# Softmax attention: the relative bias reaches the maxima through VectorE, the key tiles take another order, and the relative product is issued behind S^T

## The chip, the cores and the metric

The kernel runs on one core of a Trainium2 chip. The metric is the device time of one execution in microseconds (us). It is one launch of a two-layer network; the change touches only the softmax attention of the second layer.

## What is computed

Each layer adds an attention and a mixture of experts to its input. The attention of the second layer has 2 batches of 16 heads of size 8 over 1024 tokens, with a relative bias that depends on the clipped distance of key and query:

```
q, k, v = x @ Wq.T, x @ Wk.T, x @ Wv.T            # per head, size 8
att_rel_pos = einsum('bhsd,pd->bhsp', q, pos_emb_k)
att_idxs = clip(key - query, -128, 127) % 256
att_pos = att_rel_pos[:, :, query, att_idxs]
att = softmax((q @ k.T + att_pos) / sqrt(8), axis=-1)
y = (att @ v) @ Wproj.T
```

The distance is clipped at 128, so outside a band of three tiles of 128 keys around each tile of 128 queries the bias is one number per query and side. The kernel puts that constant into the product itself (two versions of the keys, `ka` and `kb`, one for either side) and adds the part that varies only inside the band.

## The kernel before

`softmax_attention` walks 256 slots, 16 for each of 16 pairs of heads. Three jobs run in each slot, shifted against each other.

- **R**, the relative product of row `r = n + 26` (`offsets`, L855): 24 rows by 384 columns into `rel_ps`. ScalarE copies it to `rel_sb` (L967). SyncE writes it to memory (L762) and reads it back skewed into `rel_raw` (L775), a ring of 16 rows.
- **S**, the scores of slot `m = n + 14` (`scores`, L873): a tile of 128 queries against half of the keys, two heads of 512 columns, in one of three pairs of PSUM banks (`duo`). VectorE takes the maximum of each head's 512 columns (L1009) into `part`. After 8 slots L1014 joins the two halves to `negmax`, TensorE turns it (L954), VectorE saves it (L1020), and SyncE writes it as a 25th row of `q`.
- **T**, the transposed scores S^T of slot `n` (`turned`, L900): a tile of 128 keys, in the order of `KEYS`, against half of the queries. The 25th row takes the maximum off. `turned_band` (L912) adds the band by transposing pieces of `rel_raw`. ScalarE takes the exponential (L971), and two slots later `values` (L927) multiplies it with v.

S needs the bias before its maximum. Before, `scores_band` (L887) did this on TensorE, ahead of the scores: an identity product of `rel_raw` into the banks of the next slot's S, and the scores were added on top. 10 of 16 slots have such a band, of 1 to 3 tiles for each head; in T 10 of 16 slots have one too, of 2, 4 or 6 transposes.

The banks are handed out in the order S, T, S, T over three pairs. So T of a slot waits until VectorE has reduced S of the slot before, and S waits for the exponential of two slots before (`free_pair`, L840). TensorE's order in a slot is R, S, T, T's bands, S's bands for the next slot, values. R, S and T use 24 or 25 rows of the array, in a quarter of it that depends on the head and on whether the pair is even or odd; for slots 6 to 15 of a pair R lies in the same quarters as T, for 2 to 5 in the same as S. The experts' gate choice (`choose`) is cut into steps that VectorE does in every second slot at the start.

Of the kernel before, what the change touches and what calls it, by code (L numbers as in the profile page):

```python
# [22 lines left out]
P = 128  # L23
# [623 lines left out]
def softmax_attention(nc, d, sb, scr, router):  # L647
# [9 lines left out]
    RING = 16  # L657
    KEYS = ((5, 0, 6, 1, 7, 2, 4, 3), (4, 0, 5, 1, 6, 2, 7, 3))
    with ExitStack() as ctx:
        def tile(name, shape, dt=F32):  # L660
            return ctx.enter_context(nc.sbuf_tensor("a1_" + name, shape, dt))

        def sem(name):
# [7 lines left out]
        rel_raw = tile("rel_raw", [P, RING, 2, BAND])  # L671
        part = tile("part", [P, 2, 2, 2, 4])
        negmax = tile("negmax", [P, 2, 2, 4])
# [12 lines left out]
                                                                sem("zeroed"), sem("ones_ready"))  # L686
        guarded = sem("guarded")
        qk_loaded = [sem(f"qk_loaded{s}") for s in range(4)]
# [36 lines left out]
        def bank_pair(kind, index):  # L725
            return duo[job_of[kind, index] % 3]

        banks = [duo[c // 2][:, c % 2 * CH:(c % 2 + 1) * CH] for c in range(NC)]
# [60 lines left out]
        def _(pool):  # L789
# [4 lines left out]
            pool.memset(f32(kb[:]), 1.0).then_inc(ones_ready, 1)  # L794
            pool.memset(vs[:], 0.0).then_inc(cleared, 1)
            pool.wait_ge(cleared, 2)
            pool.memset(vs[:, :, :, :, HD:2 * HD], 1.0).then_inc(cleared, 1)
# [40 lines left out]
        def _(pe):  # L838
# [18 lines left out]

            def has_band(j, x):
                return max(j - 1, 4 * x) < min(j + 2, 4 * x + 4)

            def scores(m):
                pair, j, x = m // 16, m % 16 // 2, m % 2
                out = bank_pair("s", m)
                edge = min(max(j + 2, 4 * x), 4 * x + 4)
                fresh = not has_band(j, x)
                if fresh:
                    free_pair("s", m)
                for kv, a, b in ((kb, edge, 4 * x + 4), (ka, 4 * x, edge)):
                    if a < b:
                        for hd in range(2):  # L870
                            to = rows(pair, hd, K3)
                            at = hd * CH - 4 * x * P
                            ins = pe.matmul(out[:, at + a * P:at + b * P], qs[to, home(pair), j * P:(j + 1) * P],  # L873
                                            kv[to, home(pair), a * P:b * P], start=fresh, stop=True, skip_group_check=not fresh)
                ins.then_inc(s_ready, 1)

            def scores_band(m):
                pair, j, x = m // 16, m % 16 // 2, m % 2
                if not has_band(j, x):
                    return  # L880
                a, b = max(j - 1, 4 * x), min(j + 2, 4 * x + 4)
                out, e = bank_pair("s", m), 8 * pair + j
                free_pair("s", m)
                pe.wait_ge(rel_read[e % 4], 16 * (e // 4 + 1))
                for hd in range(2):
                    at = hd * CH - 4 * x * P
                    pe.matmul(out[:, at + a * P:at + b * P], ident_r[:],  # L887
                              rel_raw[:, e % RING, hd, (a - j + 1) * P:(b - j + 1) * P].bitcast(F32R),
                              start=True, stop=True, skip_group_check=True)

# [41 lines left out]
            for n in slots:  # L932
                m, r, h = n + LS, n + LR, (n + LS - 2) // 8
                if (m - 3) % 8 == 7 and 0 <= m - 3 < SLOTS:
                    pe.wait_ge(row_saved, (m - 3) // 8 + 1)
                if r < SLOTS:
                    offsets(r)
                if 0 <= m < SLOTS:
                    scores(m)
                if 0 <= n < SLOTS:  # L940
                    if n % 8 == 0:
                        pe.wait_ge(row_stored[n // 8 % 2], 32 * (n // 16 + 1))
                    free_pair("t", n)
                    t_last = turned(n)
                if 0 <= n < SLOTS:
                    (turned_band(n) or t_last).then_inc(st_ready, 1)
                if 0 <= m + 1 < SLOTS:
                    scores_band(m + 1)
                if (m - 2) % 8 == 7 and 0 <= m - 2 < SLOTS:
# [25 lines left out]
        def _(dve):  # L975
# [15 lines left out]

            choosing = choose(router, sb, dve, then, router.biased)

            for n in slots:
# [11 lines left out]
                if 0 <= m < SLOTS:  # L1006
                    dve.wait_ge(s_ready, m + 1)
                    h, j, x = m // 8, m % 16 // 2, m % 2
                    dve.tensor_reduce(part[:, h % 2, x, :, j % 4], bank_pair("s", m)[:].rearrange("p (h t) -> p h t", h=2),  # L1009
                                      AX.X, ALU.max, negate=True).then_inc(part_ready, 1)  # L1010
                    if m % 8 == 7:
                        dve.wait_ge(part_ready, m + 1)
                        wait(dve, row_ready, h - 1)
                        dve.tensor_tensor(negmax[:, h % 2, :, :], part[:, h % 2, 0, :, :], part[:, h % 2, 1, :, :], ALU.min).then_inc(max_ready, 1)  # L1014
                if (m - 2) % 8 == 7 and 0 <= m - 2 < SLOTS:
# [418 lines left out]
```

## Time and profile before

| what | value |
|---|---|
| median of 3 runs | 1406.43 us (1398.53 to 1409.87) |
| the profiled execution's own time | 1408.63 us |
| its span in the trace | 1406.8 us |
| TensorE busy, share of the span | 84% |
| ScalarE, VectorE, GpSimd busy | 54%, 51%, 39% |
| mean granted TensorE clock | 0.911 |
| softmax attention, first R to last exponential | 535 to 1098 us |

Busy shares are averages over stages that have different limits; the change is worth what its own stage makes of it. A busy TensorE counts matmuls that overlap, so its share says that it was never long without work, not that it is at its peak. The idle time ahead of a load of weights is named by what ended it; "issue" means that the profile shows no one to wait for.

### The profile page before, as it was taken

The numbers are of one execution on the slowest core, as the hardware profiler recorded it, in microseconds if no ns is written. First come the engines' busy times: TensorE is split into PE (matmuls) and PEld (weight loads), VectorE is DVE, ScalarE is ACT, GpSimd is POOL, SyncE is SP. The second block draws the span as 40 slices with busy tenths as digits, with TensorE's granted clock in tenths as the row PEclk, the third lists the DMA queues.
The fourth block names the chain that finished last, engine by engine and source line by source line (L and its number), as shares of the span: only waits on it lengthen the run. The fifth ranks groups of instructions, "written<-read, shape, count | busy, mean of one in ns | idle before, by whom it ended". The sixth has DMA issues, their size and how long they took to land. (4 is left out here: it accounts for less than half of the span.)

```text
span 1406.8 us, 23122 instructions
## 1 busy us (share of the span) xinstructions
PE 1181.4 (84%) x8332; PEld 727.0 (52%) x8332; DVE 719.5 (51%) x998; ACT 761.5 (54%) x1136; POOL 550.8 (39%) x725
## 2 busy tenths in 40 slices
PE   3599996789986622899999999999999378898897
PEld 3233332567764521455555555555554256677685
DVE  5122221345556520676666666666664036575656
ACT  1388885644442101475777777777775255344443
POOL 1255553745443010033333333333322367454554
PEclk9999998899997555597999999999999689999999
DMA  3311101300000273877788888788761241000001
GB/s 114 149 43 49 42 31 60 105 0 0 0 0 6 82 253 111 270 188 206 185 222 227 215 235 226 223 222 224 225 206 28 81 142 29 0 0 0 0 0 30
DMA packets 119933, 155.76 MB, mean 111 GB/s; under 512 B 27806, under 2 KB 110880, under 8 KB 119840
## 3 DMA queue, kind: packets, MB, share of 16 engines
q1 hardware_dynamic: 101280, 145.30, 33.1%
q0 software_dynamic: 18560, 9.23, 4.4%
q8 instruction: 57, 0.93, 0.3%
q14 instruction: 36, 0.29, 0.1%
HBM read 81.97 MB, written 72.34 MB: 110 GB/s over the span
## 5 line engine op out<-in xcount | busy, mean ns | idle before, releaser
L1009 DVE TENSOR_REDUCE a_part<-a_duo 128x2 f32<-128x1024 f32 x256 | 311.5, 1225 | 196.3 <-PE a_duo L873 195.0
L971 ACT ACTIVATE a_probs<-a_duo 128x1024 f32<-128x1024 f32 x256 | 261.8, 1023 | 105.1 <-PE a_duo L912 99.0
L1251 POOL TENSOR_TENSOR f_hid_lo<-f_hid,f_hid_hi 128x512 fp32r<-128x512 f32 (+1 forms) x168 | 216.8, 1292 | 202.3 <-ACT f_hid_hi L1232 202.3
L818 POOL DMA_DIRECT2D scr_y1c<-a_y x256 | 132.0, 524 | 320.8 <-DVE a_y L1000 319.6
L967 ACT ACTIVATE a_rel<-a_rel_ps 128x384 f32<-128x384 f32 x256 | 126.0, 492 | 135.4 <-PE a_rel_ps L855 114.8
L623 ACT ACTIVATE a_probs<-a_duo 128x1024 f32<-128x1024 f32 x192 | 147.8, 813 | 36.0 <-PE a_duo L581 34.5
L927 PE MATMUL a_acc_ps<-a_probs,a_v 128*32 128x256 f32 x2048 | 166.9, 398 | 0.3 <-issue 0.2
L855 PE MATMUL a_rel_ps<-a_emb_all,a_q 24*128 24x384 f32 x256 | 121.0, 473 | 53.8 <-DMA a_kb<-scr_kb 31.0
L855 PEld LDWEIGHTS a_rel_ps<-a_emb_all,a_q 24*128 24x128 f32 x256 | 50.2, 196 | 161.6 <-issue 97.5
L570 POOL TENSOR_TENSOR a_probs<-a_probs,const 128x256 f32<-128x256 f32 x128 | 95.2, 763 | 86.7 <-ACT a_probs L623 86.7
L1226 ACT ACTIVATE f_gate<-f_g 128x512 f32<-128x512 f32 (+1 forms) x100 | 59.7, 597 | 121.0 <-PE f_g L1167 120.8
L1302 DVE TENSOR_TENSOR f_hid<-f_c,f_up 128x512 f32<-128x512 f32 (+1 forms) x168 | 116.1, 691 | 8.5 <-POOL f_hid_lo L1251 2.9
L1298 DVE TENSOR_TENSOR f_up<-f_u,f_gate 128x512 f32<-128x512 f32 (+1 forms) x100 | 68.8, 688 | 100.8 <-PE f_c L1172 84.1
L1232 ACT ACTIVATE f_hid_hi<-f_hid 128x512 fp32r<-128x512 f32 (+1 forms) x168 | 104.7, 623 | 24.5 <-DVE f_hid L1302 24.5
L601 PE MATMUL a_acc<-a_probs,a_v 128*32 128x256 f32 (+1 forms) x1280 | 116.3, 379 | 0.1
L912 PE MATMUL a_duo<-const,a_rel_raw 128*128 128x128 f32 x704 | 114.5, 290 | 0.0
L900 PE MATMUL a_duo<-a_q,a_ka 25*128 25x512 f32 (+3 forms) x416 | 104.0, 404 | 2.0 <-DMA a_q<-a_rows 0.7
L1165 PE MATMUL f_g<-x_hi,f_w_hi 128*128 (+1 forms) x168 | 69.4, 413 | 37.7 <-ACTq L1236 21.1
L581 PE MATMUL a_duo<-a_q,a_k 24*128 24x512 f32 (+3 forms) x384 | 86.3, 449 | 16.4 <-DMA a_k<-scr_k 15.1
L873 PE MATMUL a_duo<-a_ka,a_q 24*128 24x512 f32 (+3 forms) x416 | 99.1, 444 | 0.7 <-DVE a_rows L1020 0.7
L1179 PE MATMUL f_y<-f_hid_hi,f_w_hi 128*128 128x512 f32 (+1 forms) x168 | 69.7, 415 | 33.9 <-POOL f_hid_lo L1251 33.9
L912 PEld LDWEIGHTS a_duo<-const,a_rel_raw 128*128 128x128 f32 x704 | 75.8, 143 | 36.9 <-issue 30.5
(199 smaller groups left out, 2032.8 us busy)
## 6 DMA issues: line engine op xcount, KB each, us to landing
scr_rel<-a_rel SPq DMA_DIRECT2D x128, 384.0 KB, 3.9
a_rel_raw<-scr_rel SPq DMA_DIRECT2D x128, 384.0 KB, 4.3
f_raw<-in_w SPq DMA_DIRECT2D x33, 192.0 KB, 2.7
scr_q<-q_hi SPq DMA_DIRECT2D x4, 1024.0 KB, 7.9
scr_y1c<-a_y POOLq DMA_DIRECT2D x256, 8.0 KB, 3.4
a_q<-scr_q SPq DMA_DIRECT2D x40, 96.0 KB
a_k<-scr_k SPq DMA_DIRECT2D x32, 96.0 KB
a_q<-scr_q POOLq DMA_DIRECT2D x24, 96.0 KB, 5.4
```

Source lines behind the costliest of these rows:

```text
L601: ins = pe.matmul(acc[h % 2][to:to + 32, lo:QUARTER], vs[:, pair % 2, hd, kt, :], probs[:, n % KEPT, hd, c * QUARTER + lo:(c + 1) * QUARTE ...
L623: act.activation(probs[:, n % KEPT, :, lo:HALF], duo[n % 3][:, :, lo:HALF], ACT.Sigmoid, scale=SCALE).then_inc(sig_done, 1)
L818: pool.dma_start(scr["y1c"][w, b, head, :, at:at + QUARTER], ys[32 * (2 * hd + c) + HD * w:32 * (2 * hd + c) + HD * (w + 1), h % 2, :]).th ...
L855: pe.matmul(rel_ps[:, 0:BAND], qs[to, home(pair), j * P:(j + 1) * P], emb_all[to, :], start=True, stop=True).then_inc(rel_ready, 1)
L912: ins = pe.matmul(out[:, at:at + P], rel_raw[:, (8 * pair + j) % RING, hd, c:c + P], ident, is_transpose=True, start=False, stop=True, ski ...
L927: ins = pe.matmul(acc[to:to + 32, 0:QUARTER], vs[:, pair % 2, hd, kt, :], probs[:, n % 4, at:at + QUARTER], start=(n % 8 == 0), stop=(n % ...
L967: act.activation(rel_sb[:, e % 4, r % 2, :], rel_ps[:, 0:BAND], ACT.Copy).then_inc(saved_act, 1)
L971: act.activation(probs[:, n % 4, :], bank_pair("t", n)[:], ACT.Exp, scale=SCALE).then_inc(exp_done, 1)
L1009: dve.tensor_reduce(part[:, h % 2, x, :, j % 4], bank_pair("s", m)[:].rearrange("p (h t) -> p h t", h=2), AX.X, ALU.max, negate=True).then ...
L1232: act.activation(hid_hi[0:m, c_ % 4, :], hid[0:m, c_ % 2, :], ACT.Copy).then_inc(hi_ready, 1)
L1251: pool.tensor_tensor(hid_lo[0:m, c % 4, :], hid[0:m, c % 2, :], f32(hid_hi[0:m, c % 4, :]), ALU.subtract).then_inc(lo_ready, 1)
L1302: dve.tensor_tensor(hid[0:m, c % 2, :], w, up[0:m, c % 2, :], ALU.mult).then_inc(hid_ready, 1)
```

## The change

The identity products of the band are gone from TensorE. VectorE adds the bias while it reduces: for each head of a slot with a band one `tensor_tensor_reduce` over the band's columns (sum of S in PSUM and `rel_raw` in SBUF, negated, minimum into a third or fourth entry of `part`), then one `tensor_reduce` over the columns outside the band. `part` is filled with 3e38 once, and the join over 8 slots reduces four entries instead of two. S of a slot now always waits for its banks itself. The order of the key tiles changes, which changes which slots of T have bands. In slots from 0 on R is issued behind T and ahead of T's bands.

```
-    KEYS = ((5, 0, 6, 1, 7, 2, 4, 3), (4, 0, 5, 1, 6, 2, 7, 3))
+    KEYS = ((5, 0, 1, 6, 2, 7, 3, 4), (4, 0, 3, 5, 1, 6, 2, 7))
...
-        part = tile("part", [P, 2, 2, 2, 4])
+        part = tile("part", [P, 2, 4, 2, 4])
+        band_sum = tile("band_sum", [P, 2, 2, BAND])
...
+        def band(j, x):
+            return max(j - 1, 4 * x), min(j + 2, 4 * x + 4)
...
+            pool.memset(part[:], 3.0e38).then_inc(part_filled, 1)
...
             def scores(m):
...
-                fresh = not has_band(j, x)
-                if fresh:
-                    free_pair("s", m)
+                free_pair("s", m)
...
-                                            kv[to, home(pair), a * P:b * P], start=fresh, stop=True, skip_group_check=not fresh)
+                                            kv[to, home(pair), a * P:b * P], start=True, stop=True)
...
-            def scores_band(m):
...
-                if r < SLOTS:
+                if r < SLOTS and n < 0:
                     offsets(r)
...
                     t_last = turned(n)
+                if r < SLOTS and n >= 0:
+                    offsets(r)
                 if 0 <= n < SLOTS:
                     (turned_band(n) or t_last).then_inc(st_ready, 1)
-                if 0 <= m + 1 < SLOTS:
-                    scores_band(m + 1)
...
                     dve.wait_ge(s_ready, m + 1)
+                    a, b = band(j, x)
+                    both = bank_pair("s", m)[:].rearrange("p (h t) -> p h t", h=2)
+                    if a < b:
+                        wait(dve, part_ready, m - 1)
+                        dve.wait_ge(rel_read[e % 4], 16 * (e // 4 + 1))
+                        kind = 3 if x == 1 and j <= 4 else 2
+                        for hd in range(2):
+                            wide = (b - a) * P
+                            ins = dve.tensor_tensor_reduce(band_sum[:, m % 2, hd, 0:wide], both[:, hd, (a - 4 * x) * P:(b - 4 * x) * P],
+                                                     rel_raw[:, e % RING, hd, (a - j + 1) * P:(b - j + 1) * P], -1.0, 3.0e38,
+                                                     ALU.add, ALU.min, part[:, h % 2, kind, hd, j % 4:j % 4 + 1])
+                        lo, hi = ((b, 4 * x + 4) if a == 4 * x else (4 * x, a))
+                        lo, hi = lo - 4 * x, hi - 4 * x
+                    else:
+                        lo, hi = 0, 4
+                    ins = dve.tensor_reduce(part[:, h % 2, x, :, j % 4], both[:, :, lo * P:hi * P],
+                                            AX.X, ALU.max, negate=True)
+                    ins.then_inc(part_ready, 1)
```

The number of transposes in T's slots 0 to 15 of a pair goes from 0, 4, 0, 6, 0, 6, 2, 4, 4, 0, 6, 0, 6, 0, 4, 2 to 0, 4, 6, 0, 6, 0, 4, 2, 4, 0, 2, 6, 0, 6, 0, 4. The slots in which an S with a band is computed are 1, 2, 4, 6, 8, 9, 10, 11, 13 and 15.

## Rows read from the trace of the kernel before

**Rows 1.** Busy time by stretch; in brackets instructions, then clock, DMA share, GB/s

```profile
562.00:588.00 26.00, 21.04 (x77) 11.36 (x77) 19.23 (x21) 9.14 (x17) 0.00 (x0) 0.50 0.91 279
...
670.00:1098.00 428.00, 414.33 (x3974) 222.26 (x3970) 273.02 (x295) 307.07 (x414) 148.01 (x288) 1.00 0.72 200
```

**Rows 2.** The exponential alone (L971) by stretch: ScalarE busy, count, clock

```profile
588.00:599.00 11.00, 4.10 (x4) 0.51 0.80 257
599.00:653.00 54.00, 26.58 (x26) 1.00 0.74 203
653.00:670.00 17.00, 6.14 (x6) 0.51 0.77 173
670.00:1075.00 405.00, 208.86 (x205) 1.00 0.76 211
```

**Rows 3.** Groups by line and shape, 750 to 1050 us

```profile
L1009 DVE TENSOR_REDUCE a_part<-a_duo 128x2 f32<-128x1024 f32 x152 | 184.8, 1225 | 93.0 <-PE a_duo L873 92.5
L971 ACT ACTIVATE a_probs<-a_duo 128x1024 f32<-128x1024 f32 x152 | 155.4, 1023 | 55.0 <-PE a_duo L912 52.9
...
L967 ACT ACTIVATE a_rel<-a_rel_ps 128x384 f32<-128x384 f32 x152 | 74.9, 492 | 26.6 <-PE a_rel_ps L855 22.1
```

**Rows 4.** Who waited for whom, 750 to 1050 us: sum, times, longest

```profile
DVE a_part L1009 <- PE a_duo L873: 92.5, 111, 1.8
...
PEld a_duo L887 <- ACT a_probs L971: 5.2, 19, 0.3
```

**Rows 5.** The instructions of L887, whole run: ns min/median/max, forms

```profile
L887 PE MATMUL a_duo<-a_rel_raw,a_ident_r x320: 272/338/688, 562.5 to 1074.9; 128*128 128x256 f32 x64, 128*128 128x384 f32 x64, 128*128 128x128 f32 x32
```

**Rows 6.** TensorE's weight loads in order of time, slots 12 to 15 of a pair

```profile
908.47 0.18 PEld L855 LDWEIGHTS a_rel_ps<-a_emb_all,a_q 24*128 24x128 f32 x1 [0.54 <-DVE a_rows L1020]
...
909.12 0.64 PEld L912 LDWEIGHTS a_duo<-const,a_rel_raw 128*128 128x128 f32 x6 [0.19 <-issue]
909.73 0.30 PEld L887 LDWEIGHTS a_duo<-a_rel_raw,a_ident_r 128*128 128x128 f32 x2
910.29 0.16 PEld L927 LDWEIGHTS a_acc_ps<-a_probs,a_v 128*32 128x32 f32 x8 [0.25 <-issue]
910.86 0.18 PEld L855 LDWEIGHTS a_rel_ps<-a_emb_all,a_q 24*128 24x128 f32 x1 [0.41 <-issue]
...
912.03 0.18 PEld L855 LDWEIGHTS a_rel_ps<-a_emb_all,a_q 24*128 24x128 f32 x1 [0.41 <-ACT a_rel L967]
...
912.73 0.18 PEld L900 LDWEIGHTS a_duo<-a_q,a_kb 25*128 25x128 f32 x2 [0.52 <-DVE a_part L1009]
...
913.16 0.42 PEld L912 LDWEIGHTS a_duo<-const,a_rel_raw 128*128 128x128 f32 x4
...
915.28 0.20 PEld L912 LDWEIGHTS a_duo<-const,a_rel_raw 128*128 128x128 f32 x2 [0.31 <-issue]
915.64 0.16 PEld L927 LDWEIGHTS a_acc_ps<-a_probs,a_v 128*32 128x32 f32 x8 [0.17 <-issue]
```

**Rows 7.** The same in the last pair, where no S is left

```profile
1089.44 0.64 PEld L912 LDWEIGHTS a_duo<-const,a_rel_raw 128*128 128x128 f32 x6 [0.24 <-issue]
1090.24 0.16 PEld L927 LDWEIGHTS a_acc_ps<-a_probs,a_v 128*32 128x32 f32 x8 [0.17 <-issue]
```

**Rows 8.** The same, slot 11 of a pair, with the turn of the maxima

```profile
874.84 0.18 PEld L855 LDWEIGHTS a_rel_ps<-a_emb_all,a_q 24*128 24x128 f32 x1 [0.41 <-issue]
...
875.93 0.08 PEld L954 LDWEIGHTS a_rel_ps<-const,a_negmax 128*8 128x8 f32 x1 [0.79 <-issue]
```

**Rows 9.** VectorE in order of time, two steps of the gate choice

```profile
643.80 1.31 DVE L156 MAX8 r_top<-r_masked 128x8 f32<-128x16 f32 x16
...
648.29 0.08 DVE L160 MATCH_VALUE_LOAD r_topi<-r_top,r_masked 128x8 f32 x1
```

**Rows 10.** The instructions of L1302, PSUM and SBUF in, whole run

```profile
L1302 DVE TENSOR_TENSOR f_hid<-f_c,f_up x168: 687/691/693, 257.1 to 1395.5; 128x512 f32<-128x512 f32 x164, 96x512 f32<-96x512 f32 x4
```

**Rows 11.** DMA issues by line, 750 to 1050 us: KB each, us to landing

```profile
a_rel_raw<-scr_rel SPq DMA_DIRECT2D x77, 384.0 KB, 4.2
```

More of the change, by code:

```diff
@@ L686, in softmax_attention @@
                                                                 sem("zeroed"), sem("ones_ready"))
-        guarded = sem("guarded")
+        guarded, part_filled = sem("guarded"), sem("part_filled")
         qk_loaded = [sem(f"qk_loaded{s}") for s in range(4)]
@@ L856, in offsets @@
                           start=True, stop=True).then_inc(rel_ready, 1)
-            def has_band(j, x):
-                return max(j - 1, 4 * x) < min(j + 2, 4 * x + 4)
             def scores(m):
@@ L873, in scores @@
                             ins = pe.matmul(out[:, at + a * P:at + b * P], qs[to, home(pair), j * P:(j + 1) * P],
-                                            kv[to, home(pair), a * P:b * P], start=fresh, stop=True, skip_group_check=not fresh)
+                                            kv[to, home(pair), a * P:b * P], start=True, stop=True)
                 ins.then_inc(s_ready, 1)
-            def scores_band(m):
[L878 to L889, printed above, removed]
             def turned(n):
@@ L992, in _ @@
             choosing = choose(router, sb, dve, then, router.biased)
+            dve.wait_ge(part_filled, 1)
             for n in slots:
@@ L1007, in _ @@
                     dve.wait_ge(s_ready, m + 1)
-                    h, j, x = m // 8, m % 16 // 2, m % 2
-                    dve.tensor_reduce(part[:, h % 2, x, :, j % 4], bank_pair("s", m)[:].rearrange("p (h t) -> p h t", h=2),
-                                      AX.X, ALU.max, negate=True).then_inc(part_ready, 1)
+                    h, j, x, e = m // 8, m % 16 // 2, m % 2, m // 2
+                    a, b = band(j, x)
[16 more added lines that the diff above has]
+                    ins.then_inc(part_ready, 1)
                     if m % 8 == 7:
@@ L1013, in _ @@
                         wait(dve, row_ready, h - 1)
-                        dve.tensor_tensor(negmax[:, h % 2, :, :], part[:, h % 2, 0, :, :], part[:, h % 2, 1, :, :], ALU.min).then_inc(max_ready, 1)
+                        dve.tensor_reduce(negmax[:, h % 2, :, :].rearrange("p a b -> p (a b)"),
+                                          part[:, h % 2, :, :, :].rearrange("p k a b -> p (a b) k"), AX.X, ALU.min).then_inc(max_ready, 1)
                 if (m - 2) % 8 == 7 and 0 <= m - 2 < SLOTS:
```

## The prediction

> **What bounds the kernel now.** First the busy time by stretch, to see which engine never rests in the stage that changes. From 670 us to the end of the stage TensorE is busy for 414.3 of 428 us, at the full clock; VectorE and ScalarE are at 64% and 72% [rows 1]. Then the exponential alone, because there is one in each slot: 205 in 405 us at the full clock is 1.98 us a slot, 31.6 us for the 16 slots of a pair [rows 2]. Then the groups: in a slot ScalarE has 1.023 + 0.492 = 1.52 us of work and VectorE 1.225 us [rows 3], so both have room on average. Last the order in time, which shows that "TensorE is busy" is not all: where a slot is short, T waits for VectorE. In slot 14 R is issued at 912.03 and T at 912.73, 1.87 us after the slot before began, which is when the reduction of that slot's S is done [rows 6]. So the slot is set by TensorE's own work, with a floor under two slots in a row that VectorE's reduction draws. The change takes from the first and adds to the second.
>
> **TensorE's work after the change.** A slot without bands lasts 1.17 us (910.86 to 912.03) [rows 6]. Two transposes add 0.36 (915.28 to 915.64) [rows 6], six add 0.80 (1089.44 to 1090.24) [rows 7], four lie half way, 0.58. So the lengths are 1.17, 1.53, 1.75 and 1.97 us. After the change a pair has six slots of the first kind, two of the second and four each of the others: 7.0 + 3.1 + 7.0 + 7.9 = 25.0 us. What the identity products cost is less than their busy time: with six transposes the values start 1.17 us after the first transpose (909.12 to 910.29) [rows 6], without identity products 0.80 [rows 7], so the largest form (384 columns, 4 of 10 in a pair, [rows 5]) saves 0.37. The forms of 256 and 128 columns stream 0.11 us less each for two products at 2.4 GHz: 0.26 and 0.15. Sum for a pair: 4 x 0.37 + 4 x 0.26 + 2 x 0.15 = 2.8 us, not the 6.8 us that 20 x 338 ns would say [rows 5].
>
> **VectorE's work after the change.** 1024 columns take 1225 ns [rows 3], 512 columns from PSUM and SBUF 691 ns [rows 10]: 1.04 ns a column and 0.16 us fixed, for one source or two. The columns stay the same. A slot with a band has three instructions in place of one. Unwaited instructions follow each other faster than their durations: 16 MAX8 of 16 columns in 1.31 us, 0.08 each and 0.07 without their columns [rows 9]. Each extra one costs 0.07 to 0.16; I take 0.07, as they follow without a wait. The reduction also hands out an accumulator, which the trace of before never does on VectorE. Bounds: nothing (it is part of the instruction), or a small instruction each, 0.08 as the MATCH_VALUE_LOAD ahead of its index search [rows 9]; I take 0.08. A banded slot then has 1.23 + 2 x 0.07 + 2 x 0.08 = 1.53 us, bounds 1.23 and 1.71. The Trainium skill (VectorE: DVE Perf Modes, Two Vector instructions with no wait between them) says that an op that also writes out its accumulator is two instructions; by that rule the 0.08 is right, and without it the banded slot would be 1.37 us and the sum some 5 us better.
>
> **The slots, walked through.** T of the next slot can go 1.87 us after a slot begins when its S has no band [rows 6], 2.17 when it has one. A late T costs 0.17 less than it is late where R has gone ahead of it (T late by 0.70, and the bands start 0.43 behind T instead of 0.65 behind the slot's start [rows 6], a loss of about 0.5). With R behind T this cover stays in slots 0 to 5, where R uses other rows than T, and goes in 6 to 15. Slot by slot, each the length above plus what the slot before leaves to wait: 1.17, 2.28, 1.97, 1.20, 2.47, 1.17, 2.45, 1.53, 2.09, 1.25, 2.45, 1.97, 1.37, 2.47, 1.17, 2.45, sum 29.5 us. The same walk before: 25.0 + 2.8 + 2.2 of waits (0.53 in slots 3, 5 and 14, 0.1 to 0.2 in four others) = 30.0, measured 31.6. The 1.6 left over is the turn of the maxima (slot 11 waits until 1.09 us for it [rows 8] and is 0.8 longer) and the identity products' own wait for the exponential, 5.2 us in 9.5 pairs, 0.5 a pair [rows 4]. The second goes; the turn waits for R's copy, and R is later, so 0.1 comes back: 1.2. **After: 30.7 a pair, 0.9 less.** The new key order moves heavy T slots beside banded S slots, which is in the walk: VectorE's 2.17 us fall on slots of 1.75 or 1.97 us in 8 of 10 cases.
>
> **Moved and added waits.** R behind T: behind R on TensorE stand T's bands and the values; ScalarE copies R before its exponential, so in the six slots without bands the exponential starts about 0.67 us later. ScalarE then has 24.2 + 4.0 = 28.2 us in 30.7, covered. SyncE's write and read of `rel_raw` follow the copy; R runs 12 slots ahead of S, and the read lands in 4.2 us [rows 11], so VectorE's new wait for `rel_read` costs nothing; if that cover went, it would hold T behind it. The wait on `part_ready` is for an instruction two slots back, free. The fill of `part` and the wider join (32 instead of 16 values, 16 times) are nothing. What the gate choice asks of VectorE (MAX8 and index search, [rows 9]) now meets a fuller engine: +1 us.
>
> **The sum.** 205 + 26 slots at the full clock are 14.4 pairs [rows 2]: 14.4 x 0.9 = -13. In 28 us at half the clock TensorE is the bound (10 slots, 2.8 us each) [rows 2]; a tenth of it is identity products: -3. In the start (562 to 588 us, half clock, 14 S [rows 1]) they cost up to 0.7 us a slot, but the DMA engines are at 0.91 there with 279 GB/s, so most is not to be had: -2. With the +1: -17 us. Against the profiled execution, 1408.6 us, that is 1391.6. It stands 2.2 us above the median, so in the median's terms **1389 us**.
>
> **Rivals.**
> 1. *The waits are not formed* (chance 0.15). VectorE's three instructions cost 1.37 us, and R behind T hides as well as before. The walk gives 28.3 + 1.2 = 29.5 a pair: -30, -4 for the rest, 1372 us. For it: nothing in the trace prices R behind T. Against: slots of 1.17 us still stand before six others.
> 2. *The banded reduction is dear, and VectorE becomes the bound* (0.18). One mechanism, in the ten banded slots: the sum with bias and minimum streams slower than one column in 1.04 ns, or its accumulator costs an instruction of 0.16. At two cycles a column the mean 563 band columns add 0.59 us, and the walk gives 33.4 + 1.2: +43, 1445 us. It decides from about 1.85 us a banded slot, where the pair is back at 31.6 plus what the start gives; at 2.0 us I get 1420. Against: two sources run at full rate [rows 10].
> 3. *ScalarE's order takes over* (0.12). The exponential that is held back by R's copy lets S of two slots later go late. The pair stays near 31.3: 1402 us.
> 4. *The clock* (0.10). At the full clock TensorE was 97% busy, in the start at half clock 81% [rows 1]. After the change it rests more. 17 us at half clock held 6 slots, which take 11.9 at full: 5.1 us lost [rows 2]. Three such stretches more give 1404 us. The Trainium skill (TensorE: Matmul & The Clock Gate, Part 4) says that transposes don't count as busy for the clock in the same way; by that rule the change takes away work that counted and leaves work that doesn't, which makes this rival likelier. The trace neither shows nor excludes it.
>
> My forecast holds 0.45, between 1380 and 1398. About 1% is what a measurement of this kernel can tell from no change. Below 1392 lie three quarters of the forecast, rival 1 and a little of the rest: faster 0.50. Above 1420.5 lie most of rival 2 and a little of rival 4: slower 0.18. No change: 0.32. The range from 1368 to 1420 leaves out the far part of rival 2 and the tail of rival 1.
>
> **What would show it.** In the trace after: no L887; the new reductions at 1.04 ns a column with 0.16 us fixed (128, 256, 384 columns: 0.29, 0.42, 0.56 us), and beside them a small record each if the accumulator is one; 205 exponentials in 393 instead of 405 us; VectorE at about 75% in this stretch; TensorE waiting for VectorE at T more often than before and by up to 0.9 us in slot 10. I am wrong if the new reductions take over twice that, if exponentials come 1.98 us apart again with ScalarE's copy as the releaser, or if the granted clock falls below 1.0 after 670 us.

## The result: slower, and TensorE's clock is the reason

The changed kernel takes 1435.71 us (median of 4 executions, 1416.75 to 1443.86) against 1402.48 us before (1398.06 to 1409.87). The ratio is 1.0155, 95% interval [1.0091, 1.0218]. Ratios here and below leave out the slowest executions, here the two in which the granted clock was lowest (0.843 and 0.858); the two that it keeps had 0.868 and 0.883, where the kernel before had 0.891 to 0.922 over 19 executions, so they lose by the same cause, only less of it. The profiled execution took 1438.66 us, with a span of 1436.8 us and a mean granted clock of 0.858 (before: 1406.8 us, 0.911).

The forecast was 1389 us. Busy time by stretch, as [rows 1], is where it fails; the clock is the number behind the five engines:

```profile
588.00:625.00 37.00, 35.72 (x216) 17.34 (x215) 19.06 (x57) 19.76 (x28) 4.34 (x8) 0.50 0.51 161
625.00:670.00 45.00, 44.33 (x270) 20.47 (x263) 26.01 (x103) 22.97 (x32) 11.86 (x23) 0.50 0.57 153
670.00:714.00 44.00, 43.33 (x261) 20.09 (x263) 24.73 (x78) 21.82 (x30) 11.86 (x23) 0.50 0.57 156
714.00:800.00 86.00, 81.65 (x784) 40.23 (x784) 65.50 (x180) 67.10 (x92) 31.48 (x61) 1.00 0.83 228
...
952.00:990.00 38.00, 37.33 (x228) 17.21 (x225) 17.69 (x50) 19.13 (x26) 11.86 (x23) 0.51 0.63 175
```

Before, the clock rose at 599 us and was down once more, from 653 to 670 us [rows 2]. Now it rises at 714 us and is down again from 952 to 990 us. TensorE is busy for 97 to 99% of the time in these stretches at half the clock: here a full engine did not bring the clock up.

The exponential alone (L957 now), as [rows 2], prices it:

```profile
600.00:714.00 114.00, 39.83 (x39) 0.50 0.54 151
714.00:952.00 238.00, 126.64 (x124) 0.99 0.83 227
952.00:990.00 38.00, 13.27 (x13) 0.51 0.63 175
990.00:1103.00 113.00, 60.06 (x59) 0.97 0.62 189
```

39 slots in 114 us is 2.92 us a slot, or 46.8 us a pair. Undisturbed pairs at the full clock last 30.15 us from exponential to exponential 16 slots later; before it was 31.6. Pair by pair, the first three last 44.0, 46.6 and 42.9 us (34.6, 35.0 and 36.7 before), +27.2 us; the eleventh and twelfth 39.1 and 36.1, +12.0; the other eleven together are 10.5 us shorter. That is +28.7 of the 30.0 us between the spans.

**The mechanism itself works, and better than forecast.** Groups of VectorE by shape, 750 to 1050 us, as [rows 3]:

```profile
L1011 DVE TENSOR_REDUCE a_part<-a_duo 128x2 f32<-128x1024 f32 x56 | 68.6, 1226 | 55.9 <-PE a_duo L873 55.9
L1004 DVE CUSTOM_DVE_ANT_0 a_band_sum<-a_duo,a_rel_raw 128x384 f32<-128x384 f32 x74 | 38.4, 555 | 10.6 <-PE a_duo L873 10.1
L1004 DVE CUSTOM_DVE_ANT_0 a_band_sum<-a_duo,a_rel_raw 128x256 f32<-128x256 f32 x76 | 29.2, 422 | 8.3 <-PE a_duo L873 8.2
...
L1004 DVE DVE_READ_ACCUMULATOR2_ANT a_part<- 128x1 f32 x185 | 15.3, 83 | 0.0
```

The sum with bias and minimum is 0.56 and 0.42 us for 384 and 256 columns, as forecast. The accumulator is an instruction of its own, of 83 ns. But in order of time one banded slot on VectorE reads:

```profile
820.75 0.56 DVE L1004 CUSTOM_DVE_ANT_0 a_band_sum<-a_duo,a_rel_raw 128x384 f32<-128x384 f32 x1 [0.76 <-PE a_duo L873]
821.24 0.08 DVE L1004 DVE_READ_ACCUMULATOR2_ANT a_part<- 128x1 f32 x1
821.24 0.55 DVE L1004 CUSTOM_DVE_ANT_0 a_band_sum<-a_duo,a_rel_raw 128x384 f32<-128x384 f32 x1
821.71 0.08 DVE L1004 DVE_READ_ACCUMULATOR2_ANT a_part<- 128x1 f32 x1
821.71 0.42 DVE L1011 TENSOR_REDUCE a_part<-a_duo 128x2 f32<-128x256 f32 x1
```

The read of the accumulator begins together with the next instruction, so it costs nothing in the sequence. From 820.75 to 822.13 the slot has 1.38 us, where the forecast had 1.53.

Who waited for whom in the same stretch, as [rows 4] (sum, times, longest), with the DMA of [rows 11] below it from the view of DMA issues:

```profile
DVE a_part L1011 <- PE a_duo L873: 55.9, 56, 2.2
DVE a_band_sum L1004 <- PE a_duo L873: 27.4, 41, 3.2
...
PEld a_duo L886 <- DVE a_part L1011: 18.8, 42, 0.6
...
PEld a_acc_ps L913 <- ACT a_probs L957: 12.2, 38, 0.4
```

```profile
a_rel_raw<-scr_rel SPq DMA_DIRECT2D x75, 384.0 KB, 4.3
```

VectorE still rests 83 us of 300, T waits for it 0.6 us at most, and the bias lands as fast as before.

TensorE's weight loads show what R behind T does at the border of a half (as [rows 6] and [rows 8]; the bracket is the idle time ahead):

```profile
940.34 0.19 PEld L873 LDWEIGHTS a_duo<-a_kb,a_q 24*128 24x128 f32 x2 [0.41 <-issue]
...
941.66 0.08 PEld L940 LDWEIGHTS a_rel_ps<-const,a_negmax 128*8 128x8 f32 x1 [1.02 <-issue]
...
949.66 0.18 PEld L873 LDWEIGHTS a_duo<-a_ka,a_q 24*128 24x128 f32 x2 [0.41 <-issue]
951.65 0.18 PEld L886 LDWEIGHTS a_duo<-a_q,a_ka 25*128 25x128 f32 x2 [1.80 <-DMA a_q<-a_rows]
951.76 0.19 PEld L860 LDWEIGHTS a_rel_ps<-a_emb_all,a_q 24*128 24x128 f32 x1
```

The turn of the maxima stands 1.32 us behind its slot's start (1.09 before, [rows 8]). T of the next half waits 1.80 us for the DMA that stores the turned rows as the 25th row of `q`, and R, the bands and the values stand behind it. The clock falls at 952.7 us. SyncE's queue shows why that DMA is late:

```profile
941.57 0.36 SPq L766 DMA_DIRECT2D scr_rel<-a_rel  x1
947.92 0.36 SPq L779 DMA_DIRECT2D a_rel_raw<-scr_rel  x1
948.33 1.21 SPq L787 DMA_DIRECT2D a_q<-a_rows  x2
```

It stands behind the read of `rel_raw`, which waits for a write to land. The same place before the change, in the pair of [rows 8]:

```profile
875.84 0.36 SPq L762 DMA_DIRECT2D scr_rel<-a_rel  x1
876.30 1.07 SPq L775 DMA_DIRECT2D a_rel_raw<-scr_rel  x1
877.43 1.21 SPq L783 DMA_DIRECT2D a_q<-a_rows  x2
```

Late writes were there before too (the longest wait of the read was 7.4 us), but T then came later in its slot, behind R, and mostly found its row.

### The profile page after: what moved, and what is told of

Read it like the earlier page. It is cut to its first block and busy times, and to the rows that moved or that the text cites. A ratio compares the mean times of both kernels' runs of the same rounds, so it can differ in the third digit from the quotient of the medians.

```text
span 1436.8 us, 23125 instructions
## 1 busy us (share of the span) xinstructions
PE 1201.9 (84%) x8012; PEld 711.1 (49%) x8012; DVE 746.2 (52%) x1638; ACT 764.0 (53%) x1136; POOL 549.8 (38%) x726
## 5 line engine op out<-in xcount | busy, mean ns | idle before, releaser
L957 ACT ACTIVATE a_probs<-a_duo 128x1024 f32<-128x1024 f32 x256 | 261.4, 1022 | 58.2 <-PE a_duo L898 51.9
L1011 DVE TENSOR_REDUCE a_part<-a_duo 128x2 f32<-128x1024 f32 (+3 forms) x256 | 218.7, 856 | 99.6 <-PE a_duo L873 99.6
L913 PE MATMUL a_acc_ps<-a_probs,a_v 128*32 128x256 f32 x2048 | 189.5, 447 | 0.1
L1004 DVE CUSTOM_DVE_ANT_0 a_band_sum<-a_duo,a_rel_raw 128x256 f32<-128x256 f32 (+2 forms) x320 | 131.4, 448 | 104.0 <-PE a_duo L873 88.7
L860 PE MATMUL a_rel_ps<-a_emb_all,a_q 24*128 24x384 f32 x256 | 109.6, 428 | 56.9 <-DMA a_kb<-scr_kb 31.2
L898 PE MATMUL a_duo<-const,a_rel_raw 128*128 128x128 f32 x704 | 132.0, 323 | 0.0
L1302 DVE TENSOR_TENSOR f_up<-f_u,f_gate 128x512 f32<-128x512 f32 (+1 forms) x100 | 68.7, 687 | 100.9 <-PE f_c L1176 83.9
L898 PEld LDWEIGHTS a_duo<-const,a_rel_raw 128*128 128x128 f32 x704 | 87.8, 160 | 45.0 <-issue 44.2
L886 PE MATMUL a_duo<-a_q,a_ka 25*128 25x512 f32 (+3 forms) x416 | 100.7, 480 | 6.2 <-DVE a_part L1011 3.4
L873 PE MATMUL a_duo<-a_ka,a_q 24*128 24x512 f32 (+3 forms) x416 | 103.9, 494 | 0.0
```

The lines of the kernel that those rows point to most:

```text
L860: pe.matmul(rel_ps[:, 0:BAND], qs[to, home(pair), j * P:(j + 1) * P], emb_all[to, :], start=True, stop=True).then_inc(rel_ready, 1)
L898: ins = pe.matmul(out[:, at:at + P], rel_raw[:, (8 * pair + j) % RING, hd, c:c + P], ident, is_transpose=True, start=False, stop=True, ski ...
L913: ins = pe.matmul(acc[to:to + 32, 0:QUARTER], vs[:, pair % 2, hd, kt, :], probs[:, n % 4, at:at + QUARTER], start=(n % 8 == 0), stop=(n % ...
L957: act.activation(probs[:, n % 4, :], bank_pair("t", n)[:], ACT.Exp, scale=SCALE).then_inc(exp_done, 1)
L1004: ins = dve.tensor_tensor_reduce(band_sum[:, m % 2, hd, 0:wide], both[:, hd, (a - 4 * x) * P:(b - 4 * x) * P], rel_raw[:, e % RING, hd, (a ...
L1011: ins = dve.tensor_reduce(part[:, h % 2, x, :, j % 4], both[:, :, lo * P:hi * P], AX.X, ALU.max, negate=True)
```

## The experiments

All are timed beside the kernel before. Times are medians of all executions. "A pair" is 16 slots at the full clock in the profiled execution, "half" the stretches of the attention at half the clock from 475 us on, leaving out those under 10 us and those behind the last S. These stretches come from one execution of each kernel, and the clock differs between executions, so the mean clock over all executions is given where it matters.

### Parts of the change

**The identity products back on TensorE**, beside the sum on VectorE; S overwrites what they write.

```
+                if 0 <= m + 1 < SLOTS:
+                    scores_band(m + 1)
```

> The changed kernel, and the 20 identity products of each pair are done again where they stood before, into the banks of the next S; S then overwrites them, so they do no useful work. Theory A (the products kept TensorE's clock up; without them it stays at half for longer): the clock is full from about 600 us as before the change, mean granted clock 0.90 or more, a pair at full clock takes 30.5 to 31.5 us, and the time falls below the changed kernel's in spite of more work, to 1385 to 1405 us. Theory B (VectorE's longer reductions and the later T cost the time, the clock only follows the idling): more work on TensorE changes nothing for the better, 1430 us or more, half clock until about 710 us.

1461.43 us, ratio 1.0331 [1.0216, 1.0446]; half: 487 to 852 us; a pair 30.7 us at the full clock, 51.9 at half. The products as such do not hold the clock up; that theory falls.

**The bias on VectorE alone** (old key order, R ahead of T).

```
-    KEYS = ((5, 0, 1, 6, 2, 7, 3, 4), (4, 0, 3, 5, 1, 6, 2, 7))
+    KEYS = ((5, 0, 6, 1, 7, 2, 4, 3), (4, 0, 5, 1, 6, 2, 7, 3))
-                if r < SLOTS and n < 0:
+                if r < SLOTS:
...
-                if r < SLOTS and n >= 0:
-                    offsets(r)
```

> Only the bias moves to VectorE: key order and place of the relative product as before. Theory A: half clock until well past 650 us and time of 1410 us or more, though a pair at full clock takes 29.9 to 30.3 us. Theory B': it was R behind T or the key order that cost the clock: with both undone the clock is as before the change and the time about 1385 us.

1408.54 us, ratio 0.9992 [0.9948, 1.0036]; a pair 30.0; half: 485 to 639 and 656 to 724 us. The kernel is no faster than before, and by the clock alone: the pair is 1.6 us shorter, but the mean clock is 0.854 over 10 executions.

**The key order alone**, in the kernel before.

> The kernel before with the new key order alone; identity products stay on TensorE. My walk of the slots gives 30.0 us a pair at full clock instead of 31.6, so 14.4 x 1.6 = 23 us less, 1380 us, and by theory A the clock is as before (full from about 600 us, mean 0.90 or more). If the walk is wrong about the order, 1400 to 1410 us. If idling of TensorE as such decides the clock, this kernel idles as little as the one before and says nothing against B.

1418.68 us, ratio 1.0087 [1.0035, 1.0139]; a pair 29.95, and yet slower; half: 480 to 585 and 640 to 736 us. At the full clock the key order alone shortens the pair as much as the whole change does (30.15), with the identity products still on TensorE.

**R ahead of T again**, the rest of the change kept.

> The changed kernel with R ahead of S again; new key order, bias on VectorE. My walk gives 29.6 us a pair at full clock, 0.5 less than the changed kernel's measured 30.15. If the clock goes by how tightly full-array work is packed, and R's place changes that little, the clock is as low as in the changed kernel (0.86) and the time 1410 to 1430 us. If R behind T is what lost the clock: 0.90 and 1375 to 1385 us.

1410.41 us over 11 executions, ratio 1.0005 [0.9975, 1.0035]. By the ratios (1.0155 with R behind T) R's place is worth some 21 us of the loss. But three of the 11 took 1580 to 1600 us, at a mean clock of 0.711 to 0.736. The profiled one is among them: half the clock from 489 to 1257 us. So R ahead of T does not by itself secure the clock, and no pair at the full clock was seen.

### What moves the clock

**Filling TensorE's waits**: two products of 256 columns into `rel_ps` ahead of T, in the six slots of a pair that follow one without transposes, where T waits for VectorE.

```
+                if n >= 1 and transposes(n - 1) == 0 and r < SLOTS:
+                    wait(pe, saved_act, r)
+                    for _ in range(2):
+                        pe.matmul(rel_ps[:, 0:256], ident_r[:], emb_all[:, 0:256], start=True, stop=True)
```

> The changed kernel, and in slots that follow one without transposes (six of 16) two useless products of the identity with 256 columns of the relative table, all 128 rows, into the banks of R before R, where TensorE waits for VectorE at full clock anyway. Theory A: they stand in for the identity products; full clock from about 600 to 650 us, a pair at full clock 30.2 to 30.6 us, 1375 to 1395 us. Theory B: at half clock nothing waits there, so they add up to 0.8 us six times a pair while the clock is down, and the time is 1435 to 1455 us.

1473.83 us, ratio 1.0206 [1.0119, 1.0293]; a pair 31.84; half: 485 to 676, 683 to 728, 745 to 823 and 840 to 864 us. At the full clock TensorE is busy for 98% of the time (870 to 1140 us) in place of 95% (1000 to 1090 us in the changed kernel): less idle time, and more half clock.

**Identity products straight behind the six transposes**, in the four slots of a pair that have six, into the banks of the next S, which overwrites them.

```
+                if n >= 0 and transposes(n) == 6 and m + 1 < SLOTS:
+                    free_pair("s", m + 1)
+                    for hd in range(2):
+                        pe.matmul(bank_pair("s", m + 1)[:, hd * CH:hd * CH + 384], ident_r[:], emb_all[:, 0:384],
+                                  start=True, stop=True, skip_group_check=True)
```

> Theory A has fallen: giving the identity products back, or fillers in light slots, made it slower and the half clock longer. Theory D: the half clock ends where full-array work is packed, as before the change, where the slots with six transposes also had the large identity products right behind them; the rises stand behind such slots. This kernel is the changed one with two useless identity products of 384 columns (a fixed table, into the next S's banks, then overwritten) straight behind the six transposes, in the four slots of a pair that have six. D: the half clock ends by 620 us or so, mean clock 0.90, a pair at full clock 31.0 to 31.5 us, in all 1395 to 1405 us. Theory B (any extra work only makes it longer): 1440 us or more, clock below 0.87.

1410.99 us, ratio 1.0035 [1.0, 1.0069]; a pair 31.5 us, yet the kernel is some 17 us faster than the changed one by the ratios (25 by the medians); half: 482.5 to 592 and 650 to 670 us; mean clock 0.904 over 10 executions, 0.863 without the products.

**The same products in four slots without transposes** (3, 5, 12 and 14).

> The control: the same eight fillers a pair, of the same size, at the same place of the slot, but in slots 3, 5, 12 and 14, which have no transposes. D: the clock stays down as long as in the changed kernel or longer, mean clock 0.86 or less, 1430 us or more. If the number of full-array products decides and not their place, it is the same as with the fillers packed.

1440.92 us, ratio 1.0259 [1.0198, 1.032]; half: 479 to 613, 670 to 780 and 834 to 845 us. The same work elsewhere brings nothing over the changed kernel in time, and its mean clock over 4 executions is 0.852. The profiled execution does rise at 613 us and not at 714, so the place of the products is not shown to decide the first rise; its clock is lost again behind a wait of T for its row of 1.21 us, for 109 us. (Two stands in the gate choice just before, of 1.13 and 1.51 us, brought no fall.)

**The gate choice cut**, its MAX8 and index search in steps of four tiles, so that no reduction of VectorE stands behind 16 of them.

```
-    for t in range(NT):
-        ins = dve.max(top[:, t, :], masked[:, t, :])
-    then(ins)
-    yield
+    for first in range(0, NT, 4):
+        for t in range(first, first + 4):
+            ins = dve.max(top[:, t, :], masked[:, t, :])
+        then(ins)
+        yield
```

> The changed kernel with the gate choice's two long steps on VectorE (16 maxima, 16 index searches, 2.4 us in one piece) cut in four each. Before the change the clock fell to half at 653 us, right behind the index search, in which TensorE had to wait for the reduction. If that stall is what makes the clock fall, a kernel that is at full clock by then keeps it: in the changed kernel, which is still at half clock at 650 us, nothing changes (1420 to 1440 us); a fall there was not the cause of its loss. If VectorE's stalls keep the clock from rising, it rises before 650 us and the time is 1400 to 1415 us.

1444.7 us (1411.96 to 1470.85 over 4 executions), mean clock 0.852; half: 482 to 663 and 901 to 932 us. These runs show no gain from it alone.

**The packed products in the first two pairs only.**

```
-                if n >= 0 and transposes(n) == 6 and m + 1 < SLOTS:
+                if 0 <= n < 32 and transposes(n) == 6 and m + 1 < SLOTS:
```

> The changed kernel with the two identity products of 384 columns straight behind the six transposes in pairs 0 and 1 only (8 slots, 16 products). The values they write are overwritten by the next S, so nothing is computed from them. Theory D1 (densely packed work is needed only to bring TensorE's clock up, and it then stays up by what the kernel does anyway): half the clock ends near 590 us as with fillers in all pairs, the later pairs take 30.2 us instead of 31.5, and 14 pairs of 1.4 us less than the 1411 us with all fillers give about 1392 us. Theory D2 (the packed work is also what keeps the clock up): it rises near 590 us and falls again later, where the changed kernel fell at 952 us too, for 40 us or more; 1405 to 1430 us. Theory N (the fillers did nothing but by luck): half the clock until about 710 us and 1436 us or more.

1432.17 us, ratio 1.0192 [1.0148, 1.0236]. The clock rises at 589 us and falls twice: 647 to 684 and 739 to 845 us. TensorE's weight loads ahead of the second fall:

```profile
736.70 0.18 PEld L873 LDWEIGHTS a_duo<-a_ka,a_q 24*128 24x128 f32 x2 [0.41 <-issue]
739.53 0.28 PEld L890 LDWEIGHTS a_duo<-a_q,a_ka 25*128 25x128 f32 x2 [2.65 <-DMA a_q<-a_rows]
```

It is the same wait of T for its row as in the changed kernel, 2.65 us long; the clock falls at 738.9 us, inside the wait, and the loads behind it have the durations of half the clock.

**The bias alone on VectorE, with these products in two pairs; and the same with the gate choice cut.**

> Only the bias on VectorE (the key order and the place of the relative product as before), with the same 16 products behind the transposes of pairs 0 and 1. In the old order these slots also hold other transposes and a pair at full clock took 30.0 us. Theory D1: the rise near 590 us and no fall but the one near 653 us; 1409 us less some 25 to 45 us more at full clock times a third of them: 1385 to 1395 us. Theory D2: a fall later than 700 us, 1400 to 1415 us. Theory N: half the clock until about 720 us, 1409 us.

1390.92 us, ratio 0.986 [0.9815, 0.9904]; half: 479 to 588 and, behind a wait of T of 1.81 us for VectorE in the gate choice, 643 to 752 us.

> As the one before, with the gate choice's MAX8 and index search each cut in four steps of four tiles, so that no TensorE wait of 2 us stands at 650 us. If that wait is what brings the clock down near 653 us, the half-clock stretch of 17 to 70 us that followed it goes, and the time is 5 to 20 us under the kernel with the uncut choice: 1375 to 1385 us with Theory D1. If the fall comes without the wait, the two are equal within 5 us.

**1375.99 us** (1368.08 to 1393.78), ratio 0.9793 [0.9755, 0.9832]: faster than both kernels. Its exponential by stretch:

```profile
488.00:597.00 109.00, 5.39 (x5) 0.50 0.65 216
597.00:1070.00 473.00, 257.59 (x252) 1.00 0.76 210
```

From 597 us on the clock stays up: 252 slots in 473 us, 30.0 us a pair.

**One packed product of 384 columns in place of two, in all pairs of the changed kernel.**

> The changed kernel with one identity product of 384 columns instead of two behind the six transposes, in all 16 pairs. Cost at full clock: half of the 1.4 us a pair, so 30.8 us a pair. If half the packed work is still enough, the clock is as with two (half of it until about 595 us and some 17 us near 650 us) and the time is 1411 less 11: 1400 us. If it is not, the clock is between that kernel's 0.904 and the changed kernel's 0.863 on average and the time 1415 to 1440 us.

1391.85 us, ratio 0.9894 [0.9852, 0.9936]; half: 480 to 613 and 654 to 691 us, the second behind a wait of 1.33 us for the gate choice. The mean clock over 6 executions is 0.910. It is enough: with this one product the changed kernel beats the kernel before by 1%.

### Whose gain it is, and which part costs

**The kernel before with both remedies** of the 1376 us kernel.

> The kernel before with the two remedies of the 1376 us kernel: two identity products of 384 columns straight behind the six transposes in pairs 0 and 1, and the gate choice cut in steps of four tiles. None of the change is in it. If the gain over the kernel before comes from the remedies alone: half the clock from 485 to about 595 us and no stretch at 654 us, which gives back 17 us at half the clock, some 6 us, and the two pairs' products cost 3 us: 1398 to 1403 us. If the remedies are what made 1376 us and the bias on VectorE nothing, it is 1376 us too. By the pair times at full clock (31.6 against 30.0 us, 13 pairs) it should be some 20 us slower than the 1376 us kernel.

1400.8 us, ratio 0.999 [0.9958, 1.0021]; a pair 31.6; half: only 489 to 598 us. Its mean clock over 12 executions is 0.914, that of the 1376 us kernel over 6 also 0.914. At an equal clock the bias on VectorE is worth 25 us in the old key order. Whether the new key order would give as much with the identity products left on TensorE (its pair was 29.95 us) no run with these remedies shows.

**One packed product and the cut in all four combinations** of key order and R's place.

> The whole change, with one identity product of 384 columns behind the six transposes in all pairs, and the gate choice cut in steps. Without the cut it took 1392 us (1378 to 1412), with 37 us at half the clock from 654 us in the profiled run. If the cut removes that stretch as it did with the bias alone, 1380 to 1385 us; if the stretch comes anyway, 1392 us.

> The bias on VectorE alone, with one identity product of 384 columns behind the six transposes in all pairs, and the gate choice cut in steps. If the clock is up from about 600 us and stays: as the 1376 us kernel (two products in two pairs) plus 14 pairs of at most 0.7 us, 1376 to 1386 us; where the products also hold off later falls, down to 1370 us. If the key order and the relative product's place are what cost, it is at least 5 us under the whole change with the same products; if not, the two are equal.

> Bias on VectorE and the new key order, the relative product ahead of S^T as before; one identity product of 384 columns behind the six transposes in all pairs, the gate choice cut. Between the kernel with both parts (1395 us) and that with neither (1380 us). If the key order is what costs, 1395 us: its slots with six transposes stand between others without any. If the relative product's place costs, 1380 us.

> Bias on VectorE and the relative product behind S^T, the old key order; the same product and cut. If the key order is what costs, 1380 us; if the relative product's place costs (it then stands between S^T and its transposes, so that the transposes no longer follow work of the same bank, and the clock is lower in the profile), 1395 us. If each part costs half, both runs come out near 1387 us.

| | R ahead of T | R behind T |
|---|---|---|
| old key order | 1380.06, ratio 0.9824 [0.978, 0.9869] | 1390.3, ratio 0.9891 [0.9845, 0.9937] |
| new key order | 1377.18, ratio 0.9819 [0.9773, 0.9865] | 1395.44, ratio 0.9937 [0.9899, 0.9975] |

R's place costs 10 and 18 us, the key order nothing that this can tell (-3 and +5). Part of R's cost is not the clock: a pair at the full clock is 30.7 us with R ahead and 30.9 behind in the old order, 30.2 and 30.8 in the new, which over some 13 pairs is 2 of the 10 and 8 of the 18 us. Half the clock after the first rise: none with R ahead; with R behind 768 to 785 us in one, 703 to 724 and 860 to 891 us in the other. Even so, one of the 12 executions of the full change with both remedies took 1526.96 us, at a mean clock of 0.798. The stretches from 768 and 860 us follow waits of T for its row of 0.78 and 1.43 us, that from 703 us the turn:

```profile
701.36 0.08 PEld L951 LDWEIGHTS a_rel_ps<-const,a_negmax 128*8 128x8 f32 x1 [1.01 <-issue]
702.30 0.18 PEld L875 LDWEIGHTS a_duo<-a_ka,a_q 24*128 24x128 f32 x2 [0.56 <-DVE a_rows L1035]
```

**T's bands by plain products in place of transposes.**

```
-                        ins = pe.matmul(out[:, at:at + P], rel_raw[:, (8 * pair + j) % RING, hd, c:c + P], ident,
-                                        is_transpose=True, start=False, stop=True, skip_group_check=True)
+                        ins = pe.matmul(out[:, at:at + P], rel_raw[:, (8 * pair + j) % RING, hd, c:c + P].bitcast(F32R), ident_r[:],
+                                        start=False, stop=True, skip_group_check=True)
```

> The changed kernel with the bias of S^T's band written by plain products against the identity in place of the transposes: as many instructions, of 128 columns each, in the same places. If transposes do not count for the clock and plain products do (the mechanism of my fourth rival), half the clock ends near 590 us instead of 714 us and the time is about 1400 us, unless a plain product of 128 columns takes longer than a transpose; if a plain one takes more than 60 ns longer, 112 of them add over 6 us a pair and the pair at full clock shows it. If the kind of instruction does not matter, half the clock lasts to about 710 us and the time is 1436 us or more.

1623.37 us, ratio 1.1586 [1.1518, 1.1655]. These instructions alone (L898), 620 to 700 us, at half the clock in both kernels; the changed kernel first:

```profile
620.00:700.00 80.00, 20.60 (x76) 13.84 (x76) 0.50 0.56 151
```

```profile
620.00:700.00 80.00, 20.93 (x76) 17.54 (x76) 0.50 0.60 152
```

The products are as many, and as long within 2%; their weight loads take longer (17.54 against 13.84 us). But the clock of the second never rises while the stage lasts, and all four executions have a mean clock of 0.695 to 0.714. Its exponential, 600 to 1300 us:

```profile
600.00:1300.00 700.00, 248.27 (x243) 0.50 0.52 140
```

### All profiles together

The profiles of the two kernels and of the 18 experiments hold 18 falls of the clock of 10 us or more between 600 us and the last S. Each begins within 2.5 us of the end of a stand of TensorE (here: idle time ahead of a weight load, under which products can still run) of 0.76 us or more: 8 behind the gate choice, 7 behind T's wait for its row, 3 behind the turn.

| | gate choice whole | gate choice cut |
|---|---|---|
| R ahead of T | 4 falls in 5 kernels, all at the choice | none in 4 kernels |
| R behind T | 10 falls in 8 kernels, 4 of them at the choice | 4 falls in 3 kernels |

Two of these kernels, R ahead again and the plain products, had no full clock to lose in this stage, and the one with the identity products back only from 852 us on. T's wait for its row stands 4 times in the 9 profiles with R ahead, 34 times in the 11 with R behind, at any length.

Such stands are far more common than falls. At the full clock, behind the first rise, the profiles hold 12 waits of T for its row of 0.76 us or more, of which 7 were followed by a fall; 10 stands in the gate choice of 1.1 us or more, of which 8 were; 7 of S in the last pair, of 1.20 to 1.36 us, none; and 193 ahead of the turn (0.78 us with R ahead, 1.01 behind), of which 3. So the order in time speaks for the first two as a cause and hardly for the turn, and no length of a stand decides alone.

The mean clock over all executions supports the packed work. In nine of the ten kernels that have it, the mean clock is 0.895 to 0.914; in the tenth, which has it in two pairs only and R behind T, it is 0.871. In the eight others with the bias on VectorE it is 0.704 to 0.863. In the kernel before it is 0.906, and 0.877 with the new key order there. After a fall the clock is back in 17 to 38 us where all pairs have packed work (5 falls), elsewhere in 10 to 109 us (13 falls, half of them 44 us or more).

## Why the prediction was wrong

**The full clock, forecast right.** "30.7 a pair, 0.9 less" was measured as 30.15, 1.45 less. Most of the difference is the accumulator, which I took at 0.08 us each and which lies over the next instruction. The Trainium skill (VectorE: DVE Perf Modes, Two Vector instructions with no wait between them) says that such an op is two instructions; the trace shows two, but the price I gave the second was wrong. Without it the prediction's own sum was "some 5 us better", or 30.35 a pair. The gain is not the removed products' alone, though: the bias by itself gives a pair of 30.0 us, the key order by itself 29.95, each about what the whole change gives, and R behind T costs 0.6 in the new order (30.8 against 30.2, with one packed product in both). Rivals 1, 2 and 3 are settled: the banded slot costs 1.38 us, which is rival 1's 1.37 and not above the 1.85 from which rival 2 decides; T waits for VectorE (L886, 42 times, 18.8 us in 300, 0.6 at most), so the waits that rival 1 leaves out are formed, and the pair lies midway between its 29.5 and the forecast; and ScalarE's exponential holds up only the values, by 0.4 us at most, so that rival 3 does not come about.

**The half clock, which failed.** The step that failed is "in 28 us at half the clock TensorE is the bound": it took the stretches at half the clock as those of before. Between 588 us and the last S they grew from 28 to 177 us. The prediction's own sign of being wrong, a granted clock below 1.0 after 670 us, came about. Rival 4 had the mechanism in name, at a chance of 0.10, and its size was off: "three such stretches more", 51 us, against 149 us more. A pair loses 13 to 16 us there and gains 1.45 elsewhere, so that ten slots at half the clock take back what six pairs gain. Its price of 5.1 us for 17 us, 0.30 a us, was nearly right: the five pairs that hold 135 of the 149 us lost 39.2 us, or 46 with the 7 that they gained by the shorter pair, 0.34 a us.

**The reason given for rival 4 fell too.** By the Trainium skill (TensorE: Matmul & The Clock Gate, Part 4) transposes don't count as busy in the same way, and I reckoned that the removed products did. No run bears this out. With the products back (and R still behind T) the half clock lasted until 852 us, and with plain products in place of the transposes it never ended. What went with a higher clock was plain work packed straight behind six transposes (0.904 over 10 executions, against 0.852 over 4 with the same work in slots without transposes).

**The new wait.** I named T's bands and values as what stands behind R, and SyncE's `rel_raw` as covered. I passed over the turn of the maxima as 0.1 us, and SyncE's third DMA, the row that T of the next half needs. It is issued five slots ahead of its use; R's copy is later, T is earlier in its slot and slots are shorter, so that a late write now reaches T. In the profiles its direct cost is small (2.6 us between 600 and 1060 us); what follows it is not: half the clock for 37 us, or 106 in the experiment with packed products in two pairs. That this wait brings the fall rests on the order in time in 7 cases and on R's place being worth 10 to 21 us, of which 2 to 8 are not the clock's; no run took the wait away alone, and 5 of 12 such waits were followed by none.

**Still open.** Why the first rise is at 714 us in the changed kernel, at 639 us with the bias alone and at 585 to 599 us with the identity products where they were. With packed work it was at 587 to 621 us in ten profiles, but with the products spread it was at 613 us too. No run separates packing from what the transposes ahead of it do, and no kernel's rise was seen in a second execution.

## What to carry to other kernels

Removing work from TensorE is a gain only as long as the granted clock stays: price a change at both clocks, ask where TensorE will stand for a microsecond, and look at the clock row before any other. When the clock is lost, compare kernels at an equal clock before judging a change (here the remedies alone gave nothing, and with the bias on VectorE 25 us). An instruction that is moved behind another takes with it the copy, the turn and the small DMA that share its queues; the one to fear is that with the shortest way from issue to use.

## What was unexpected of the hardware

- TensorE, 98% busy, stayed at half its clock (1.2 GHz) for 126 us from 588 us on, and with plain products of 128 columns for 731 us (580 to 1311 us).
- 16 identity products of 384 columns, straight behind the six transposes of the first two pairs, went with a rise at 589 us in place of 714; such products in slots without transposes, in every pair, went with one at 613 us and left the time at 1440.92 us. Adding work made the changed kernel 44 us faster (1435.7 to 1391.9 us; 37 by the ratios).
- The read of VectorE's accumulator is recorded with 83 ns and costs nothing between two instructions.
- The clock of one kernel differs between executions: 0.843 to 0.883 over 4 after the change, 0.891 to 0.922 over 19 before.
